# A graph network kernel: target ids loaded and pair lists made in four parts, three of them between the groups of the score pass

## What is computed

```
q, k, v = x @ Wq.T, x @ Wk.T, x @ Wv.T            # 8 heads of 16
scores  = einsum('ehc,ehc->eh', q[dst], k[src]) / 4 + edge_attr @ We.T
alpha   = segment_softmax(scores, dst)
out0    = segment_sum(v[src] * alpha, dst)        # layer 0
...
out1    = segment_sum(xw[dst] * coef, src)        # layer 1, graph convolution
```

## Time and profile before

| what | value |
|---|---|
| median of three runs | 2847.01 us (2846.44 to 2853.34) |
| the profiled execution | 2839.77 us, of it 2837.9 us span |
| mean granted TensorE clock | 0.85 |
| busy: PE / DVE / ACT / POOL | 1694.7 / 2100.8 / 861.3 / 1513.4 us |
| from the load of the target ids to the first combined group | 1198.33 to 1270.92 us |
| score pass on DVE | 1270.92 to 1505.87 us |
| POOL's stores of counts | 1256.99 to 1915.86 us |

### The profile page before, as it was taken

The page is one execution under the profiler, slowest core; times in us unless marked ns, Lnnn a source line. Parts: engine busy times, 40 slices in busy tenths (PEclk is TensorE's granted clock), DMA queues, the critical chain, the costliest instruction groups (busy, mean ns, idle before and its releaser), DMA issues. The chain is left out here.

```text
span 2837.9 us, 41359 instructions
## 1 busy us (share of the span) xinstructions
PE 1694.7 (60%) x11847; PEld 1217.0 (43%) x11847; DVE 2100.8 (74%) x4613; ACT 861.3 (30%) x2233; POOL 1513.4 (53%) x1545
## 2 busy tenths in 40 slices
PE   5333322235666666427773585785115878997998
PEld 4222211224444444326773475442111227996664
DVE  8888766647787778538989787512778997877998
ACT  0111111112233333213332354001015874554444
POOL 0777777747777777626777777767510004550000
PEclk9999999997667577658986797998557998997999
DMA  8566665649888888799991684795775645872764
GB/s 305 170 186 193 183 187 142 182 103 225 230 243 237 240 234 241 176 73 210 233 214 23 149 195 93 204 276 120 299 298 226 231 162 112 189 145 72 214 193 136
DMA packets 706227, 535.20 MB, mean 189 GB/s; under 512 B 397687, under 2 KB 656311, under 8 KB 694401
## 3 DMA queue, kind: packets, MB, share of 16 engines
q1 hardware_dynamic: 642325, 412.92, 57.8%
q0 software_dynamic: 59552, 102.50, 10.2%
q10 hardware_dynamic: 4136, 17.13, 1.6%
HBM read 371.29 MB, written 161.06 MB: 188 GB/s over the span
## 5 line engine op out<-in xcount | busy, mean ns | idle before, releaser
L689 POOL DMA_INDIRECT adjacency<-gm_slot,slot_tmp x440 | 454.2, 1032 | 230.8 <-issue 88.5
L1373 POOL DMA_INDIRECT table<-pay_own,stage x432 | 415.1, 961 | 232.6 <-issue 120.5
L1373 POOL DMA_INDIRECT table<-q,stage x424 | 409.3, 965 | 133.0 <-issue 118.0
L1335 PE MATMUL banks<-acc,work 128*128 128x26 bf16 (+1 forms) x856 | 82.8, 227 | 447.1 <-DVE work L1329 446.9
L1601 PE MATMUL banks<-pool,both 128*128 x1320 | 255.9, 361 | 103.8 <-ACT q L1611 48.2
L2638 POOL TENSOR_TENSOR pool<-pool,raw 128x260 f32<-128x260 f32 x110 | 110.7, 1007 | 383.0 <-DMA pool<-table 299.1
L1307 DVE TENSOR_SCALAR work<-acc,pidx 128x512 bf16<-128x512 bf16 x214 | 80.7, 377 | 250.0 <-DMA acc<-low_rows_by_src 130.7
L1335 PEld LDWEIGHTS banks<-acc,work 128*128 128x128 bf16 x856 | 48.6, 112 | 505.9 <-DVE work L1329 501.1
L1325 ACT CAST work<-banks 128x104 bf16<-128x104 f32 x214 | 59.3, 277 | 622.2 <-PE banks L1317 568.4
L1601 PEld LDWEIGHTS banks<-pool,both 128*128 128x128 bf16 x1320 | 157.6, 119 | 181.1 <-issue 126.0
L2529 PE MATMUL banks<-acc,q 128*65 128x512 f32 (+1 forms) x350 | 147.1, 562 | 43.1 <-DVE acc L2516 43.1
(11 more groups left out here) (586 smaller groups left out, 4429.8 us busy)
## 6 DMA issues: line engine op xcount, KB each, us to landing
work<-adjacency SPq DMA_DIRECT2D x75, 1600.0 KB, 7.6
acc<-table SPq DMA_DIRECT2D x110, 332.0 KB, 5.3
q<-table SPq DMA_DIRECT2D x110, 256.0 KB, 4.0
pool<-table SPq DMA_DIRECT2D x220, 128.0 KB, 2.6
adjacency<-slots SPq DMA_DIRECT2D x65, 392.0 KB
work<-adjacency SPq DMA_DIRECT2D x25, 832.0 KB, 5.3
work<-adjacency SPq DMA_DIRECT2D x25, 768.0 KB, 5.0
adjacency<-slots ACTq DMA_DIRECT2D x11, 1320.0 KB
```

The lines of the kernel that those rows point to most:

```text
L689: nc.gpsimd.indirect_dma_start(adjacency, bass.IndirectOffsetOnAxis(ap=pair_at[:, t:t + 1], axis=0), pair_n[:, t:t + 1], None).then_inc(co ...
L1335: last = nc.tensor.matmul(table[:, 0:j + 1, :], oh_keys[n % 3][:, j, :], hi16[n % 4][:, j:j + 1, :].to_broadcast([P, j + 1, NH]), start=Fa ...
L1373: nc.gpsimd.indirect_dma_start(to, bass.IndirectOffsetOnAxis(ap=stage[n % 4][:, j:j + 1], axis=0), pay[n % 4][:, j, 0:width], None).then_i ...
```

## The change

The load of five words is cut in four, tiles 0 to 111, 112 to 223, 224 to 331 and 332 to 439 (`CHUNKS`). SP issues the first as before; ACT issues the other three when the first has landed and the `q` products are done. The three stages of `link_slot_ids`, `pair_counts` and the release, and the stage `slot_rows`, are gone. Their work is written per part, as pieces (`vector_codes`, `vector_runs`, `vector_carries`, `vector_totals`, `vector_pairs` and their counterparts on PE, ACT and SP). The pieces of part 0 run ahead of the score pass, those of parts 1, 2 and 3 in the steps 8 to 16, 17 to 25 and 26 to 34 of it. A row is now a tile of 128 slots; part c has 112 or 108 rows. PE turns the codes three times, shifted by one slot each way, so that a row's neighbours need no trip of their own; what runs over from part to part is carried in `ended`. The pieces use PSUM bank 7, so that the products of the scores turn over three banks (4 to 6), and `products` waits for a group later than before. POOL numbers the cells (`number_cells`) at the start of the block; `store_counts` waits ahead of each part for its lists and, ahead of parts 1 to 3, for the landing of the store before.

```diff
             def load_low(sp, n, k):
                 wait(sp, s_oh, n - 3)
+                if n * G in CHUNK0:
+                    sp.wait_ge(s_low_written[CHUNK0.index(n * G)], 16)
                 sp.dma_start(lows[k % 4], row_for_all("by_dst", n)).then_inc(s_lr[k % 4], 16)
...
-                wait(pe, s_pr, n - 3)
+                wait(pe, s_pr, n - 2)
                 for j in range(G):
-                    last = nc.tensor.matmul(ps[4 + k % 4][:, j * P:(j + 1) * P], oh[k % 2][:, j, :],
+                    last = nc.tensor.matmul(ps[4 + n % 3][:, j * P:(j + 1) * P], oh[k % 2][:, j, :],
                                             q_nodes[:, bass.ds(blocks[j], 1), :].rearrange("p o d -> p (o d)"),
                                             start=True, stop=True)
...
-                nc.vector.tensor_tensor(prod[k % 2][:, :, :], ps[4 + k % 4][:, :].rearrange("p (g n) -> p g n", g=G),
+                nc.vector.tensor_tensor(prod[k % 2][:, :, :], ps[4 + n % 3][:, :].rearrange("p (g n) -> p g n", g=G),
...
-            return {"sync": [(0, load), (0, load_low)], "vector": [(5, combine), (2, onehots)],
-                    "scalar": [(4, keep_bias), (2, copies), (0, pack)], "tensor": [(3, products), (1, transposes)]}
...
+            return {"sync": [(0, load), (0, load_low), (0, lists["sync"])], "vector": [(5, combine), (2, onehots), (0, lists["vector"])],
+                    "scalar": [(4, keep_bias), (2, copies), (0, pack), (0, lists["scalar"])],
+                    "tensor": [(3, products), (1, transposes), (0, lists["tensor"])]}
...
+        def link_slot_ids(link, o, highs, lows, t0=0, t1=T):
...
-        def pair_counts():
...
-                    for k in range(4):
-                        nc.tensor.transpose(ps[4 + k][:, 0:SR], run_s[:, k * P:(k + 1) * P], ident[0:SR, 0:SR]).then_inc(s_b, 1)
-
+        CHUNK0 = [0, 112, 224, 332]
+        CHUNKS = list(zip(CHUNK0, CHUNK0[1:] + [T]))
+        CHUNK_GROUP = [None, 8, 17, 26]
+        s_chunk = [lasting_sem(f"target_ids_loaded{c}") for c in range(len(CHUNKS))]
+        s_low_written = [lasting_sem(f"target_lows_written{c}") for c in range(len(CHUNKS))]
+        s_pairs = lasting_sem("pairs_ready")
+
+        def load_chunk(eng, c):
+            t0, t1 = CHUNKS[c]
+            with nc.allow_non_contiguous_dma(reason="five numbers of each row"):
+                eng.dma_start(back2[:, t0:t1, :], table2[t0 * P:t1 * P, C_ID:C_GE + 1].rearrange("(t p) c -> p t c", p=P)) \
+                   .then_inc(s_chunk[c], 16)
+
+        slot_cell = [work[0:t1 - t0, 512 + c * P:512 + (c + 1) * P] for c, (t0, t1) in enumerate(CHUNKS)]
+        s_cells = lasting_sem("slot_cells_made")
+
+        def number_cells(g):
+            for c, (t0, t1) in enumerate(CHUNKS):
+                nc.gpsimd.iota(slot_cell[c], [[1, P]], base=CELLS + t0 * P, channel_multiplier=P,
+                               allow_small_or_imprecise_dtypes=True).then_inc(s_cells, 1)
...
+            def vector_codes(v, c):
+                if not chain:
+                    chain.append(Chain(v, s_v))
+                    blocks_counted(v)
+                    nc.vector.memset(through[:, 0:1], 0.0)
+                    nc.vector.memset(ended[:, 0:1], 0.0)
+                    chain[0].link(nc.vector.memset(code, -1.0))
+                link, (t0, t1) = chain[0].link, CHUNKS[c]
+                v.wait_ge(s_chunk[c], 16)
+                wait(v, s_turned, c)
+                link_slot_ids(link, "dst", back2[:, t0:t1, 1], back2[:, t0:t1, 0], t0, t1)
+                nc.vector.tensor_copy(ge["dst"][:, t0:t1], back2[:, t0:t1, 4])
+                part = code[:, 1 + t0:1 + t1]
+                link(nc.vector.scalar_tensor_tensor(out=part, in0=back2[:, t0:t1, 3], scalar=float(P), in1=back2[:, t0:t1, 2],
+                                                    op0=ALU.mult, op1=ALU.add))
+                link(nc.vector.tensor_scalar(part, part, -float(P), 0.0, ALU.add, ALU.max))
+                link(nc.vector.scalar_tensor_tensor(out=part, in0=node["dst"][:, t0:t1], scalar=float(NPAD), in1=part,
+                                                    op0=ALU.mult, op1=ALU.add))
+                marks["codes", c] = chain[0].k
+
...
+                nc.tensor.transpose(before[0:R, :], code[:, t0:t1], ident[:, :])
+                nc.tensor.transpose(behind[0:R, :], code[:, 2 + t0:2 + t1], ident[:, :]).then_inc(s_turned, 1)
+
+            def scalar_lows(act, c):
+                R = CHUNKS[c][1] - CHUNKS[c][0]
+                act.wait_ge(s_low, c + 1)
+                nc.scalar.copy(low16[c][0:R, :], lows[0:R, :]).then_inc(s_low_kept, 1)
+
+            def sync_lows(sp, c):
+                t0, t1 = CHUNKS[c]
+                sp.wait_ge(s_low_kept, c + 1)
+                sp.dma_start(low_rows["by_dst"][t0 * P:t1 * P].rearrange("(r n) -> r n", n=P), low16[c][0:t1 - t0, :]) \
...
+                link(nc.vector.tensor_tensor(la[:, 0:P - 1], at[:, 0:P - 1], at[:, 1:P], ALU.not_equal))
+                wide_one = ones[0:R, 0:1].to_broadcast([R, P])
+                nc.vector.tensor_tensor_scan(ru, kp, wide_one, 0.0, ALU.mult, ALU.add)
+                link(nc.vector.tensor_tensor_scan(pr, wide_one, kp, 1.0, ALU.mult, ALU.min))
+                nc.vector.tensor_copy(end[0:R, 0:1], ru[:, P - 1:P])
+                link(nc.vector.tensor_copy(end[0:R, 1:2], pr[:, P - 1:P]))
+                marks["ends", c] = chain[0].k
...
+            def vector_pairs(v, c):
+                t0, t1 = CHUNKS[c]
+                v.wait_ge(s_back, 2 * c + 2)
+                nc.vector.tensor_copy(pair_at[:, t0:t1], back[0][:, 0:t1 - t0])
+                chain[0].link(nc.vector.tensor_copy(pair_n[:, t0:t1], back[1][:, 0:t1 - t0]))
+                v.sem_inc(s_pairs, 1)
+
+            def begin(*parts):
+                return lambda eng: [part(eng, 0) for part in parts]
+
+            def at_groups(parts):
+                def todo(eng, n, k):
+                    for c in range(1, len(CHUNKS)):
+                        for lag, part in parts:
+                            if n == CHUNK_GROUP[c] + lag:
+                                part(eng, c)
+                return todo
+
+            def first_chunk_and_loads(act):
+                act.wait_ge(s_chunk[0], 16)
+                for c in range(1, len(CHUNKS)):
+                    load_chunk(act, c)
+                scalar_lows(act, 0)
+
+            return ({"vector": begin(vector_codes, vector_runs, vector_carries, vector_totals, vector_pairs),
+                     "tensor": begin(tensor_lows, tensor_turns, tensor_ends, tensor_enters, tensor_back),
+                     "scalar": first_chunk_and_loads, "sync": begin(sync_lows)},
+                    {"vector": at_groups([(0, vector_codes), (2, vector_runs), (4, vector_carries), (6, vector_totals), (8, vector_pairs)]),
+                     "tensor": at_groups([(0, tensor_lows), (1, tensor_turns), (3, tensor_ends), (5, tensor_enters), (7, tensor_back)]),
+                     "scalar": at_groups([(0, scalar_lows)]), "sync": at_groups([(3, sync_lows)])})
+
+        back2 = pay_own[:, :, :, :].rearrange("p k g n -> p (k g n)")[:, 0:5 * T].rearrange("p (t c) -> p t c", c=5)
         UNDER_WAY = 7
         IN_TURN = UNDER_WAY + 1
         TURN_SHIFT = IN_TURN.bit_length() - 1
@@ -683,6 +762,10 @@
         def store_counts(g, t0, t1, keep_pace):
 
             for t in range(t0, t1):
+                if t in CHUNK0:
+                    g.wait_ge(s_pairs, CHUNK0.index(t) + 1)
+                    if t:
+                        g.wait_ge(counted_in[(t - 1) % IN_TURN], 16 * ((t - 1) // IN_TURN + 1))
                 keep_pace(g, t)
                 if t >= UNDER_WAY:
                     g.wait_ge(counted_in[(t - UNDER_WAY) % IN_TURN], 16 * ((t - UNDER_WAY) // IN_TURN + 1))
...
             @block.sync
             def _(sp):
-                with nc.allow_non_contiguous_dma(reason="five numbers of each row"):
-                    sp.dma_start(back2, table2[0:P * T, C_ID:C_GE + 1].rearrange("(t p) c -> p t c", p=P)).then_inc(s_rb2, 16)
+                load_chunk(sp, 0)
+
+            @block.gpsimd
+            def _(g):
+                counts_and_node_sums(g)
         node_products("q", lambda b: xs[:, b, :], D, wqkv[:, 0:D], take_q)
-        s_sl = sem("target_slot_ids")
-        with next_stage() as block:
-            @block.vector
-            def _(v):
-                v.wait_ge(s_rb2, 16)
-                link_slot_ids(Chain(v, s_sl).link, "dst", back2[:, :, 1], back2[:, :, 0])
-        pair_counts()
-        s_sr, s_gm, s_pa = lasting_sem("slot_sums_written"), lasting_sem("node_maxima_gathered"), sem("pairs_ready")
+        s_sr, s_gm = lasting_sem("slot_sums_written"), lasting_sem("node_maxima_gathered")
...
@@ -1753,7 +1830,7 @@
 
         def counts_and_node_sums(g):
 
-            g.wait_ge(s_pa, 1)
+            number_cells(g)
             store_counts(g, 0, BEFORE_SUMS, pace_of_scores)
             g.wait_ge(s_sr, 16)
```

(26 more changed lines are left out.)

161 lines of the change are left out of this document (71 added, 90 removed).

## The result

| | before | changed | ratio, 95% interval |
|---|---|---|---|
| median, first chip | 2845.11 us (8 runs) | 2828.78 us (8 runs) | 0.9939 [0.9923, 0.9955] |
| median, second chip | 2829.53 us (23 runs) | 2817.37 us (12 runs) | 0.9955 [0.9941, 0.9970] |
| profiled execution | 2839.77 us | 2831.07 us, of it 2829.3 us span | |
| mean granted TensorE clock | 0.85 | 0.858 | |

The change makes the kernel faster by 13 to 17 us, about 15 (the mean of the two ratios, 0.9947, of 2830 us). The forecast was 15 us. Its sum came out right, but the terms for the start of both chains and for POOL's waits did not.

What follows compares the result with a forecast made beforehand. Two chains started by the pair lists, through DVE and through POOL, were taken to end the block nearly together; main chain 43.2 - 24 - 3 = 16 us, POOL 33.9 - 18 = 16, smaller 15: 2832 us, range 2821 to 2847.

Steps and rivals of the forecast that it cites:

- The wait for the load: Between `q` products and scores: part 0's load lands before the products end, so DVE's 24.43 us of idle time go.
- The lists of part 0: Ahead of the scores: part 0's list work, with small instructions and trips to PE, takes 11.5 us, ending at 1222.7.
- Parts 1 to 3 on DMA: In the scores: 27.5 us of loads nearly all hidden, with 3 us of stall at part 1.
- Start of the scores: First one-hots to first combine takes 5 us; first combine at 1227.7 against 1270.92, 43.2 us gained.
- Parts 1 to 3 on DVE: In the score pass: the later parts' lists add 24 us to DVE, all of it charged.
- rival (a): In the scores: loads not hidden, all 27.5 us land on the scores, slower at 2855 us; chance 0.10.
- POOL: POOL's store chain: starts 33.9 us earlier, loses 18 us to three landing waits of 6 each, gains 16 us.
- Rival (b): POOL decides the block's end, landings take 9 to 10 us each, no change: 2843 us; chance 0.19.
- The sum: At the block's end: main chain and POOL each gain 16 us, the smaller is 15, giving 2832 us.

Runs made afterwards that it cites:

- e2: Changed kernel with only part 1's load issued ahead of ACT's rounding, part 2's in step 8 and part 3's in step 17; ratio to the kernel before 0.9918, again 0.9899.
- a0: The changed kernel measured once more, unaltered, on the second chip; ratio to the kernel before 0.9955.
- e1: Changed kernel with ACT rounding part 0's low parts before it issues the three loads; ratio to the kernel before 0.9936.
- e3: Changed kernel with three more POOL waits for the store just issued, at tiles 56, 168 and 280; ratio to the kernel before 1.0019.
- e5: Changed kernel with each part's last tile stored eighth from its end and the three waits for the store just issued dropped; ratio to the kernel before 0.9926.

## Why the prediction was right, step by step

- **The wait for the load.** Right: no idle time at the first read, part 0 landed after 10.5 us (said: 9.4 and some 2).
- **The lists of part 0.** The work was right, the time was not. From 1207.66 to 1233.42 are 25.8 us. Less the 15.45 us of waiting, and with the 1.06 us that the same trip takes in e2, it is 11.4; said were 11.5. **This is the step that failed:** it had nothing for ACT's three issues, which stand ahead of the rounding in `first_chunk_and_loads`. "Parts 1 to 3 on DMA" priced their transfer and its share of the 16 engines, not ACT's time while it issues. That cost 16.1 us at the first combine and 13.6 us at POOL's start.
- **Start of the scores.** 7.2 us from the first one-hots to the first combine instead of 5, since SP's first row load stood behind the same rounding: in e2, where it didn't, it is 5.0. Together: the first combine gained 25.9 us, not 43.2.
- **Parts 1 to 3 on DVE.** Right: DVE's busy time between first combine and the end of the scores rose from 207.0 to 229.2 us, by 22.2. The stretch itself took 235.1 us before and 258.5 after, 23.4 more where 24 were said; in a0 it took 253.7, only 18.6 more than in the one profile of before.
- **Parts 1 to 3 on DMA, rival (a).** The 3 us of stall at part 1 didn't come: DVE reads part 1 at 1249.59 with no idle time. The wait ahead of the multiplication is 16.5 us over 110 groups (18.2 over 107 before), the DMA share 0.84 (0.90). Rival (a) is excluded. The Trainium skill ("DMA: Bandwidth & Descriptors", section "Issuing engines are not separate DMA queues") is not contradicted: such loads do slow each other, as part 1's shows, which landed after 20.9 us in e2 beside the rows and after 11.9 us without them. There was room for it.
- **POOL.** Its start came 20.0 us earlier, not 33.9 (ACT's issues). Its three waits cost 4.9, 1.6 and 1.6 us above the usual 0.3, in all 8 instead of 18. Net of these 12, where 16 were said; the last gather came 9.6 us earlier in the profile. Rival (b), landings of 9 to 10 us each, did not happen. But its other half did: POOL decides the end, by 4.8 us, a slack that the prediction left open ("somewhere in 1982 to 1986").
- **The sum.** DVE's chain had gained only 25.9 - 23.4 = 2.5 us at the end of the scores. It reached the norm 9.5 us earlier. The other 7.0 us lie in stretches that the change does not touch and whose length varies from profile to profile (softmax to norm: 472 us before, 454 to 471 in the other twelve). On POOL's side two errors cancelled: the issues on ACT took some 14 us off its gain, and its waits gave back 10, so 12 were left of 16. On DVE's side nothing cancelled: 2.5 us stand against 16, and that the time fell by 15 all the same is explained only as far as the slack of 4.8 us goes; the rest is open, as said at the table. That the forecast of 15 us was met is therefore luck in good part. The sign, the place of the gain, the work on DVE and the hidden loads were right for the reasons given.

## What to carry to other kernels

Count the issuing of a DMA as work of its engine, and look at what stands behind it in that engine's program. Here DMAs of many small pieces, issued back to back, held the engine for most of the time that the loads ahead took; issued when the last had landed, they took 0.4 us each. Where two chains meet at a stage's end, find the fixed distance from each to the next start in the profile. It tells which is last and how much slack the other has, and so what an edit on either can be worth.

## What was not expected of the hardware

- **Issuing blocks.** A DMA of 14336 pieces of 20 bytes took 0.41 us to issue on an idle queue and 8.67 us behind another of its kind (27.7 us for three beside the rows' loads). The second issue ended 2.8 us before the load ahead of it landed, which took 11.9 us; in e1, where that load took 21.4 us, the second issue took 17.4 us and ended 3.5 us before it. So the issue goes with the load ahead of it; that it waits for room on the queue is an inference. The same section of the Trainium skill says that the time to initiate a DMA is usually small relative to the DMA itself; here it is 8.67 us for a load of which one by itself lands in 10.5 us, and the measurement decides.
- **One load by itself** of this kind lands in 10.5 us, and in 20.9 beside row loads, without the scores being slower for it.
- **A landing** of an indirect store that POOL waits for costs more where DMA is busy. Above the usual gap of 0.3 us it cost 4.9 us at a DMA share of 0.94 and 1.6 us at shares of 0.01 and 0.02 in the changed kernel; in e3 it cost 3.6 to 8.5 us at shares of 0.70 and more. It does not follow the share alone: 8.5 us stand at 0.78, 3.6 at 1.07.
- **DVE holds POOL.** In e5 one gather took 3.53 us instead of 0.94, beside the only wide DVE instruction of the place:

```profile
1936.07 3.49 DVE L2280 SCALAR_TENSOR_TENSOR xs<-acc,xs 128x3200 f32<-128x3200 f32 x1
```

```profile
1936.86 3.53 POOL L2036 DMA_INDIRECT both<-late_rows,first_slot_dst  x1 [0.30 <-issue]
```

Both end within 0.9 us of each other. It costs POOL's chain 2.6 us at the end of the block. All 13 profiles show it at this place (3.09 to 4.19 us), that of the kernel before too (3.27), and all show it once more, on a store beside the wide addition ahead of the first norm (3.39 to 3.99): the store at 1741.47 above took 3.59 us. That DVE is the cause is inferred from the coincidence; no run takes the wide instruction away.
